# A windowed-attention layer on one core: q normed by GpSimd ahead of its transpose, epsilon inside the sums, all probabilities normed by GpSimd, another order of the work

## What is computed

```python
h = layernorm(x)
q = rmsnorm((h @ wq.T).reshape(B, T, 16, 64), q_norm_w)     # 16 heads of 64
k = rmsnorm((h @ wk.T).reshape(B, T, 4, 64), k_norm_w)      # 4 kv heads, each serves 4 q heads
v = (h @ wv.T).reshape(B, T, 4, 64)
scores = q @ k.T / 8, with key j seen by query i only where i >= j and i - j < 128
x = x + (softmax(scores) @ v) @ wo.T
h = layernorm(x)
gate = softmax(h @ gate_w.T)                                # 8 experts
x = x + h @ weight.T + (1/16) * sum_e gate_e * lora_V_e @ (lora_U_e @ h)
```

## Time and profile before

| | us |
|---|---|
| median of 3 runs | 2232.22 |
| lowest and highest of them | 2228.25, 2237.21 |
| the profiled execution | 2228.48 |
| its span, first to last instruction | 2226.6 |

### The profile page before, as it was taken

How to read it: one execution, slowest core, us unless ns; L and a number is a source line. 1 busy time by engine, 2 the same in 40 slices (tenths; PEclk the granted TensorE clock), 3 DMA queues, 4 the chain that set the end, 5 groups by cost and what they waited for, 6 DMA issues and landing times.

```text
span 2226.6 us, 108163 instructions
## 1 busy us (share of the span) xinstructions
PE 2078.9 (93%) x42768; PEld 1703.3 (76%) x42768; DVE 2036.1 (91%) x8486; ACT 1840.6 (83%) x6663; POOL 1162.5 (52%) x1036
## 2 busy tenths in 40 slices
PE   7999999999999998999999999999999999999996
PEld 4777777777777777777877777777777877777775
DVE  7999998999999998999999999999999999999995
ACT  6888888888888887888888888888888888888884
POOL 3555554555555555555555555555555555555552
PEclk9999999999999999999999999999999999999998
DMA  3111111111111111111111111111111111111110
GB/s 99 44 51 48 51 52 46 50 49 52 47 49 48 52 48 48 49 51 47 50 54 47 49 50 51 50 48 52 47 50 50 52 49 49 48 51 50 49 43 24
DMA packets 138198, 110.88 MB, mean 50 GB/s; under 512 B 37216, under 2 KB 136928, under 8 KB 137696
## 3 DMA queue, kind: packets, MB, share of 16 engines
q1 hardware_dynamic: 137696, 103.97, 17.1%
...
## 4 chain that ended last, share of the span: by engine, by line
PE 61%; DVE 25%; issue 9%; ACT 4%; DMA 0%; DVEq 0%; POOL 0%; SPq 0%
PE ps_y L730 12%; PE ps_scores L714 10%; DVE soft L498 10%; PE ps_y L662 7%; PE ps_y L663 7%; PE ps_y L664 7%; PE ps_y L668 6%; DVE pT L516 6%; PE ps_f L668 3%; DVE yT_l L522 2%; ACT soft L357 2%; PE ps_e L662 2%; PE ps_e L663 2%; PE ps_e L664 2%; PE ps_f L662 2%
## 5 line engine op out<-in xcount | busy, mean ns | idle before, releaser
L348 ACT ACTIVATE soft<-soft,neg_max 128x160 f32<-128x160 f32 x2048 | 848.7, 419 | 0.2 <-DVE neg_max L498 0.2
L275 POOL TENSOR_TENSOR soft<-soft,rden 128x640 f32<-128x640 f32 x384 | 482.0, 1255 | 393.0 <-DVE rden L505 393.0
L264 POOL TENSOR_TENSOR q_r<-q_ve,minus_half 128x8 f32<-128x8 f32 x256 | 420.4, 1642 | 316.3 <-DVE q_ve L485 303.8
L498 DVE CUSTOM_DVE_ANT_0 soft<-ps_scores,mask_band,q_r 128x160 f32<-128x160 f32 x1536 | 495.8, 378 | 37.6 <-PE ps_scores L714 28.1
L516 DVE STREAM_TRANSPOSE pT<-soft 128x640 f32<-128x640 f32 x512 | 415.7, 831 | 96.5 <-PE ps_y L730 91.6
L714 PE MATMUL ps_scores<-kT,qT 64*32 64x160 f32 (+4 forms) x16384 | 395.0, 286 | 36.9 <-issue 27.9
L730 PE MATMUL ps_y<-pT,v_rep 32*64 32x128 f32 x17920 | 329.7, 275 | 79.1 <-issue 77.5
L348 ACT ACTIVATION_READ_ACCUMULATOR soft<-soft,neg_max 128x1 f32 x2048 | 393.5, 192 | 0.0
L730 PEld LDWEIGHTS ps_y<-pT,v_rep 32*64 32x64 f32 x17920 | 284.4, 130 | 120.9 <-issue 119.1
L714 PEld LDWEIGHTS ps_scores<-kT,qT 64*32 64x32 f32 x16384 | 228.4, 106 | 155.8 <-issue 121.4
L363 ACT ACTIVATE yT_h<-ps_y 128x512 fp32r<-128x512 f32 x256 | 139.1, 595 | 228.1 <-PE ps_y L730 228.1
...
## 6 DMA issues: line engine op xcount, KB each, us to landing
v_rep<-v_own SPq DMA_DIRECT2D x2048, 32.0 KB, 1.9
xs<-x SPq DMA_DIRECT2D x128, 128.0 KB, 2.4
out<-ob SPq DMA_DIRECT2D x128, 128.0 KB, 2.1
...
nw<-norm_w SPq DMA_DIRECT2D x1, 1.0 KB, 6.0
```

What stands on the lines that cost most here:

```text
L264: pool.tensor_tensor(q_r[:, T % DEEP, c], q_ve[:, T % DEEP, c], minus_half[:, 0:8], ALU.pow).then_inc(s_qr[n], 1)
L275: pool.tensor_tensor(soft[:, r], soft[:, r], rden[:, r].unsqueeze(2).to_broadcast([P, REP, SPAN]), ALU.mult).then_inc(s_pn, 1)
L348: last = nc.scalar.activation(soft[:, r, h], soft[:, r, h], ACT.Exp, bias=neg_max[:, r, h:h + 1], scale=-1.0, accum_out=den[:, r, h:h + 1])
L498: last = nc.vector.tensor_tensor_reduce(soft[:, r, h], ps_scores[:, h, 0:SPAN], mask_band[:] if slot(T) else mask_first[:], q_r[:, T % DEE ...
```

## The change

It does this:

- After `copy_q`, GpSimd multiplies q in SBUF by its factor, 8 heads (128x512) at a time (`norm_q`), and only then is q transposed. `mask_and_max` no longer takes `q_r` and has the constant 1.0 in its place.
- The squares of q and k lie in one tensor `squares` with 65 columns per head. DVE writes the scaled epsilon into the 65th (`eps_squares`, 20 elements per row), so that the sum holds it. `q_mean_square`, `k_mean_square` and `x_eps` go.
- `NORM_BY_ACT` is empty: POOL norms the probabilities of all four groups.
- The lists of calls of POOL, ACT, DVE and PE are in another order, x is treated one step further ahead, and the PSUM banks are given out anew. SP's list is as it was.

The diff, cut to its core (of PE's step the new order alone, its `freed` calls left out):

```diff
-NORM_BY_ACT = (3,)
+NORM_BY_ACT = ()
...
-        x_eps = sb("x_eps", [P, DEEP, 1])
+        squares = sb("squares", [P, 2, HEADS + KV_HEADS, HD + 1])
-        k_sq, k_ms, k_ve, k_r = sb("k_sq", [P, 2, KVDIM]), sb("k_ms", [P, DEEP, KV_HEADS]), sb("k_ve", [P, DEEP, KV_HEADS]), sb("k_r", [P, DEEP, KV_HEADS])
+        k_ms, k_r = sb("k_ms", [P, DEEP, KV_HEADS]), sb("k_r", [P, DEEP, KV_HEADS])
...
-        ps_q = [ps_a, ps_c]
-        ps_qT = [ps_b, ps_c]
-        ps_kv, ps_kT, ps_xT, ps_hT, ps_tT = ps_f, ps_f, ps_a, ps_f, ps_a
-        ps_o, ps_ffn = ps_d, ps_e
+        ps_q = [ps_d, ps_f]
+        ps_qT = [ps_e, ps_b]
+        ps_kv, ps_kT, ps_xT, ps_hT, ps_tT = ps_f, ps_a, ps_b, ps_c, ps_a
+        ps_o, ps_ffn = ps_c, ps_e
...
             def k_power(T):
                 if live(T):
-                    pool.wait_ge(s_kve, done(T))
-                    pool.tensor_tensor(k_r[:, T % DEEP], k_ve[:, T % DEEP], minus_half[:, 0:KV_HEADS], ALU.pow).then_inc(s_kr, 1)
+                    pool.wait_ge(s_kms, done(T))
+                    pool.tensor_tensor(k_r[:, T % DEEP], k_ms[:, T % DEEP], minus_half[:, 0:KV_HEADS], ALU.pow).then_inc(s_kr, 1)
 
             def q_power(T, n):
                 if live(T):
                     c = slice(8 * n, 8 * n + 8)
-                    pool.wait_ge(s_qve[n], done(T))
-                    pool.tensor_tensor(q_r[:, T % DEEP, c], q_ve[:, T % DEEP, c], minus_half[:, 0:8], ALU.pow).then_inc(s_qr[n], 1)
+                    pool.wait_ge(s_qms[n], done(T))
+                    pool.tensor_tensor(q_r[:, T % DEEP, c], q_ms[:, T % DEEP, c], minus_half[:, 0:8], ALU.pow).then_inc(s_qr[n], 1)
+
+            def norm_q(T, n):
+                if live(T):
+                    q = q_raw[:, T % 2, 8 * n:8 * n + 8]
+                    pool.wait_ge(s_qr[n], done(T))
+                    pool.wait_ge(s_qc[n], done(T))
+                    pool.tensor_tensor(q, q, q_r[:, T % DEEP, 8 * n:8 * n + 8].unsqueeze(2).to_broadcast([P, 8, HD]), ALU.mult).then_inc(s_qn[n], 1)
...
             def step(T):
-                k_power(T + 1)
-                q_power(T, 1)
-                x_rstd_power(T + 2)
                 norm_probs(T, 0)
-                q_power(T + 1, 0)
+                norm_q(T + 1, 0)
+                norm_q(T + 1, 1)
+                norm_probs(T, 1)
+                x_rstd_power(T + 3)
                 h_rstd_power(T - 2)
-                norm_probs(T, 1)
+                q_power(T + 2, 0)
                 norm_probs(T, 2)
-
-            for T in range(-2, TILES + 2):
+                k_power(T + 2)
+                norm_probs(T, 3)
+                q_power(T + 2, 1)
+
+            for T in range(-3, TILES + 2):
                 step(T)
...
-                    nc.scalar.activation(k_sq[:, T % 2], ps_kv[:, 0:KVDIM], ACT.Square, scale=HD ** -0.5).then_inc(s_ksq, 1)
+                    nc.scalar.activation(squares[:, T % 2, HEADS:HEADS + KV_HEADS, 0:HD], ps_kv[:, 0:KVDIM].rearrange("p (g d) -> p g d", d=HD), ACT.Square, scale=HD ** -0.5).then_inc(s_ksq, 1)
...
-                    nc.scalar.activation(q_sq[:, T % 2, n], ps_q[n][:], ACT.Square, scale=HD ** -0.5).then_inc(s_qsq[n], 1)
+                    nc.scalar.activation(squares[:, T % 2, 8 * n:8 * n + 8, 0:HD].rearrange("p (c e) d -> p e c d", e=2),
+                                         ps_q[n][:].rearrange("p (e c d) -> p e c d", e=2, d=HD), ACT.Square, scale=HD ** -0.5).then_inc(s_qsq[n], 1)
...
             def step(T):
-                square_q(T + 2, 0)
+                exps(T - 1, 2, range(2, 4))
+                square_k(T + 1)
+                exps(T - 1, 3, range(0, 2))
+                high_x(T + 3)
+                exps(T - 1, 3, range(2, 4))
+                gate_exp(T - 3)
+                store_v(T + 1)
                 exps(T, 0, range(0, 2))
-                high_tg(T - 3)
-                store_v(T + 1)
                 exps(T, 0, range(2, 4))
...
+                square_q(T + 2, 0)
+                high_tg(T - 3)
+                store_qT(T, 1)
+                high_h(T - 2)
+                store_kT(T + 1)
+                if T == -1:
+                    high_weights(W_O, W_V)
+                copy_q(T + 2, 0)
+                exps(T, 1, range(0, 2))
                 square_q(T + 2, 1)
+                exps(T, 1, range(2, 4))
                 copy_q(T + 2, 1)
-                high_x(T + 3)
-                store_qT(T + 1, 0)
-                high_h(T - 2)
-                exps(T, 1, range(0, 2))
-                exps(T, 1, range(2, 4))
                 high_y(T - 1, 0)
                 high_y(T - 1, 1)
-                store_kT(T + 1)
+                store_qT(T + 1, 0)
                 exps(T, 2, range(0, 2))
-                exps(T, 2, range(2, 4))
-                exps(T, 3, range(0, 2))
-                gate_exp(T - 2)
-                exps(T, 3, range(2, 4))
-                square_k(T + 2)
-                store_qT(T + 1, 1)
-                if T == -1:
-                    high_weights(W_O, W_V)
-                normalise(T, 3)
-                copy_q(T + 3, 0)
...
-                    nc.vector.tensor_scalar(x_eps[:, T % DEEP], x_mv[:, T % DEEP, 1:2], RMS_EPS, LN_EPS * RMS_EPS, ALU.mult, ALU.add).then_inc(s_xeps, 1)
...
+            def eps_squares(T):
+                if live(T):
+                    dve.wait_ge(s_xmv, done(T))
+                    if live(T - 2):
+                        dve.wait_ge(s_kms, done(T - 2))
+                        dve.wait_ge(s_qms[0], done(T - 2))
+                        dve.wait_ge(s_qms[1], done(T - 2))
+                    nc.vector.tensor_scalar(squares[:, T % 2, :, HD], x_mv[:, T % DEEP, 1:2].to_broadcast([P, HEADS + KV_HEADS]), RMS_EPS, LN_EPS * RMS_EPS,
+                                            ALU.mult, ALU.add).then_inc(s_xeps, 1)
+
             def sum_k(T):
                 if live(T):
                     dve.wait_ge(s_ksq, done(T))
-                    nc.vector.reduce_sum(k_ms[:, T % DEEP], k_sq[:, T % 2].rearrange("p (h d) -> p h d", d=HD), AX.X).then_inc(s_kms, 1)
-
-            def k_mean_square(T):
-                if live(T):
-                    dve.wait_ge(s_kms, done(T))
                     dve.wait_ge(s_xeps, done(T))
-                    nc.vector.tensor_tensor(k_ve[:, T % DEEP], k_ms[:, T % DEEP], x_eps[:, T % DEEP].to_broadcast([P, KV_HEADS]), ALU.add).then_inc(s_kve, 1)
+                    nc.vector.reduce_sum(k_ms[:, T % DEEP], squares[:, T % 2, HEADS:HEADS + KV_HEADS], AX.X).then_inc(s_kms, 1)
...
             def sum_q(T, n):
                 if live(T):
                     dve.wait_ge(s_qsq[n], done(T))
-                    nc.vector.reduce_sum(q_ms[:, T % DEEP, 8 * n:8 * n + 8], q_sq[:, T % 2, n].rearrange("p (h d) -> p h d", d=HD), AX.X).then_inc(s_qms[n], 1)
-
-            def q_mean_square(T, n):
-                if live(T):
-                    c = slice(8 * n, 8 * n + 8)
-                    dve.wait_ge(s_qms[n], done(T))
                     dve.wait_ge(s_xeps, done(T))
-                    nc.vector.tensor_tensor(q_ve[:, T % DEEP, c], q_ms[:, T % DEEP, c], x_eps[:, T % DEEP].to_broadcast([P, 8]), ALU.add).then_inc(s_qve[n], 1)
+                    nc.vector.reduce_sum(q_ms[:, T % DEEP, 8 * n:8 * n + 8], squares[:, T % 2, 8 * n:8 * n + 8], AX.X).then_inc(s_qms[n], 1)
 
             def mask_and_max(T, g):
 
                 if live(T):
                     r = ring(T, g)
                     dve.wait_ge(s_s, groups(T, g))
-                    dve.wait_ge(s_qr[g // 2], done(T))
                     wait(dve, s_pt, groups(T, g) - RING)
                     if T == 0:
                         dve.wait_ge(s_mask, MASK_PARTS)
                     for h in range(REP):
-                        head = 8 * (g // 2) + 4 * (h // 2) + 2 * (g % 2) + h % 2
                         last = nc.vector.tensor_tensor_reduce(soft[:, r, h], ps_scores[:, h, 0:SPAN], mask_band[:] if slot(T) else mask_first[:],
-                                                              q_r[:, T % DEEP, head:head + 1], HIGHEST, ALU.add, ALU.min, accum_out=neg_max[:, r, h:h + 1])
+                                                              1.0, HIGHEST, ALU.add, ALU.min, accum_out=neg_max[:, r, h:h + 1])
                     last.then_inc(s_mm, 1)
...
             def step(T):
-                sum_q(T, 1)
-                k_mean_square(T)
+                eps_squares(T + 2)
+                gate_inverse(T - 4)
+                gate_share(T - 4)
+                inverse(T - 2, 3)
                 gate_t(T - 4)
                 transpose_probs(T - 2, 2)
-                transpose_probs(T - 2, 3)
-                x_mean_and_var(T + 1)
+                norm_k(T)
+                add_x(T - 3)
+                low_tg(T - 4)
                 mask_and_max(T - 1, 1)
...
-                q_mean_square(T - 1, 1)
-                low_tg(T - 4)
-                norm_k(T)
+                transpose_probs(T - 2, 3)
+                low_h(T - 3)
+                inverse(T - 1, 0)
```

(44 more changed lines are left out.)

101 lines of the change are left out of this document (42 added, 59 removed).

## The result

The changed kernel takes 2159.32 us, median of 4 runs (2156.68 to 2160.91); the kernel before, on the same chip, 2230.64 us in 4 runs. The ratio is 0.9675 [0.9651, 0.9698], so 71 us less, where 32 had been forecast. It is faster, as forecast, but the time lies 13 us under the lower end of the range. The profiled execution took 2159.75 us, its span is 2157.9 and the granted clock 0.996 of full speed, against 0.992 before.

What follows compares the result with a forecast made beforehand. PE was taken as the bound: 2228.5 us profiled, less 42 of waits, plus 5 for the order and 5 for unseen waits, gave 2196.5; with 3.7 for the median, 2200. Range 2172 to 2248, the forecast's own 2180 to 2218.

Steps and rivals of the forecast that it cites:

- What bounds the kernel: PE is the bound before and after; DVE has time to spare, its wait for `attend` rising to about 200 us.
- PE's waits, 42 less 5 us: On PE, 42 us of waits for other engines go; 5 us are left for small waits not seen.
- The order's own cost, 5 us for `transpose_tg` ahead of scores: On PE, `transpose_tg` right ahead of scores of group 1 costs 0.04 us a tile, 5 us (0 to 15).
- Start and end of the run: On PE, counted only inside the upper bound of 51 us for the waits, with no term of its own.
- DVE, 163 us less: On DVE, 183 us of operations go and 20 us of `eps_squares` come, net 163 us, 1.3 us a tile.
- The constant: On DVE, 1.0 for `q_r` in `mask_and_max` changes nothing, 0, with ends of 0.038 us each, 78 us.
- `eps_squares` not held: On DVE, `eps_squares` takes near 0.15 us, not locked out by GpSimd; at worst held 160 us in all.
- The margin of 1.1 us ahead of `attend`: From the end of scores of group 1, DVE needs 2.65 us and PE 3.75, so `attend` need not wait.
- The holes, 0 us: In PE's scores and `attend`, about 97 us of gaps from running out of instructions stay unchanged.
- the holes go: Rival: PE's gaps in small matmuls vanish, another 97 us falls away, giving 2103 us; chance 0.05.

Runs made afterwards that it cites:

- b_arith2: The new arithmetic in the order and banks of the kernel before, with GpSimd's list fitted to PE's; 2188.17 us, ratio 0.9764.
- b_const: The kernel before with the constant 1.0 for q's factor in `mask_and_max`, q's normalization left out of its scores; 2187.97 us, ratio 0.9783.
- a_ptr: The changed kernel with the constant 1.0 of `mask_and_max` given as a pointer to a column of ones; 2168.76 us, ratio 0.9699.
- a_hold2: The changed kernel with a wait on PE's own `project_q(T+2, 0)` ahead of `project_out(T-2, 1)`, far from the small matmuls; 2204.45 us, ratio 0.9835.
- a_hold: The changed kernel with a wait on PE's own `project_q(T+2, 1)` right ahead of scores of group 2; 2250.7 us, ratio 1.005.
- b_addx: The kernel before with DVE's `add_x(T-3)` called ahead of `norm_k` and `sum_q`; 2243.98 us, ratio 1.0031.
- a_actnorm: The changed kernel with the probabilities of group 3 normed by ACT again instead of POOL; 2236.48 us, ratio 1.0023.

## Why the prediction was wrong, step by step

- **What bounds the kernel**: right. PE has 93% of the chain, and DVE's wait for `attend` is 197.1 us (forecast about 200).
- **PE's waits, 42 less 5 us**: right. The count has 26 us of waits and 7 of the base. The base is a floor taken within one kernel, so it hides a delay of every tile; b_arith2, in the old order, has the same lower base, so these 7 belong to the waits: 33 us for 37.
- **The order's own cost, 5 us for `transpose_tg` ahead of scores**: too dear. The base is 1969.2 in the old order with the new arithmetic (b_arith2) and 1970.2 in the new.
- **Start and end of the run**: no term of the sum apart from the 42; 4 us were gained.
- **DVE, 163 us less**: the parts were off, the whole about right: 198 us. The constant was taken at 0, with ends of 38 ns either way; it is 58 ns, outside them, and 117 us (b_const). The rest is then 81 us, not 163. A sum of rows overstates short instructions that overlap their neighbours: with the q_ve records taken out of the trace of before, DVE's busy time falls by 106 us, not by the 145.1 of their row. Neither error reached the time by itself, as the prediction said of such ends: a_ptr is within 0.3% of the changed kernel.
- **`eps_squares` not held**: right, but not for a reason that was tested. It always ran beside a power, so whether 20 columns with one input are held beside a multiplication stays open. With one column they are not: h_ve lay wholly inside a multiplication 122 times in the kernel before and took 155 ns at most.
- **The margin of 1.1 us ahead of `attend`**: two slips of PE's side that cancel. The 0.70 us for scores of group 2 already holds the fixed 0.25 that is added again, and the 0.25 behind scores of group 1 is missing. The sum of 3.75 us stands: in the timeline of the changed kernel it is 3.7.
- **The holes, 0 us**: this is the step that failed. The prediction read them rightly as PE running out of instructions, and then took them for PE's own, "the run of small matmuls is the same". The run is the same, but the length of a hole is not a property of the run: it hangs on how early PE's instruction stream gets through what stands ahead of it. It shrank by 35 us (31.7 by the matmuls' rows), all but 5 of it through the order (138.0 in b_arith2, 107.9 after). It is nearly all of the miss. With what was measured for each term the sum is 2196.5 - 35 (holes) - 4 (start and end) - 4 (the order's cost) + 4 (waits 33 for 37) = 2157.5, against the 2159.75 of the profiled execution. As a rival, "the holes go" was given only all or nothing, 97 us with a chance of 0.05; the lower end of the range held no more than 5 to 9 us of it.

What sets the length of a hole, as far as the runs show it: for each `attend` of 160 loads I took the place, in loads from its start, where the count of PE's instructions reaches an end, and the largest gap there, as a mean over the tiles.

```
place of the end   before  b_arith2   after  a_hold2  a_hold   (ns)
 64 to  79            863       511     368      514     759
 80 to  95           1005      1129     530      483    1769
 96 to 111           1373      1292     398      432    1914
112 to 127           1661      1550    1277     1376    1743
128 to 143           1628      1678    1654     1729    1628
```

An end before load 64 leaves gaps under 0.3 us in any of them, one from 128 on about 1.6 us in all. They differ in between. An end there is 128 loads behind the end ahead of it, which lies in the work just ahead of scores of group 2. There stand the waits of PE's stream. In the kernel before, the wait of `transpose_h` for `add_x` was passed at 1021.94 us, the last one, of scores of group 2, at 1022.06, and these scores began on the array at 1022.38. In the changed kernel `project_q` stands right ahead of these scores: the stream passed the same last wait at 1006.24 us, while the array was still at the start of `project_q`, and the scores began at 1007.70. This lead of the stream (from the end of the last wait that is an instruction of its own to the start of scores of group 2) hardly varies from tile to tile. Its medians beside the holes of the count, us:

```
          lead    holes
a_hold    0.03    165.8
before    0.27    143.2
b_addx    0.32    132.7
b_arith2  0.48    138.0
a_hold2   1.40    115.8
after     1.40    107.9
a_ptr     1.40    109.0
a_actnorm 1.87    105.9
```

The link between the two is in the trace of the instruction queue. For ends at 96 to 111, the packet that was asked for last ahead of the hole starts, against the start of scores of group 2, 1.43 us later in a_hold, 0.92 later before, 0.78 later in b_arith2, 0.16 later in a_hold2, and 0.04 earlier in the changed kernel. In each, PE comes back about 1.4 us after the end of that packet. The packets themselves are no quicker: 1.14 us on average both before and after. So a hole is shorter because its packet is asked for earlier.

That holding the stream right ahead of the run lengthens the holes is shown by a_hold against a_hold2. That the longer lead shortened them in the changed kernel is read from these rows: no run changed the lead alone in the order of before. The lead is also not all of it, since b_addx has shorter holes than b_arith2 with less lead; and beyond 1.4 us more of it brings little.

On the rule that the prediction weighed: the Trainium skill, Runtime: NRT & Kernel Launch, section "Instruction fetch mechanics", has blocks of 16 KiB for 256 instructions, and the runs agree (342 packets of 16 KB for 87592 instructions). It calls the cost of crossing one "mostly hidden". In full-size work that holds here: of 60 ends that lie wholly in it in the changed kernel, 53 leave no gap over 0.3 us. In a run of small matmuls (160 loads in 2.29 us) it does not: a hole there is up to 1.9 us long.

**Open.** The orders were not taken apart engine by engine, so which call's move shortened the holes was not tried: by b_arith2 it was not the arithmetic. Why a wait on PE's own work costs 0.33 us of restart is not shown. And the fixed steps at a change of tile size (0.25, 0.17 and 0.37 us) are as large in the changed kernel (0.25, 0.17 and 0.36); nothing here tells their cause.
